# Scatters and early gathers six in a row with one wait, and the shared FFN's up-products of groups 2 to 15 as three products of high and low parts

## The reference, cut to what matters

```
gelu = lambda t: jax.nn.gelu(t, approximate=False)
shared = gelu(x @ W1s + b1s) @ W2s + b2s
rw = jax.nn.softmax(x @ Wr, axis=-1)
topw, topi = jax.lax.top_k(rw, K)                       # K = 2 of E = 8 experts
...
h = gelu(jnp.einsum('bsd,edf->bsef', x, W1p) + b1p)
priv = jnp.einsum('bsef,efd->bsed', h, W2p) + b2p
routed = jnp.einsum('bsed,bse->bsd', priv, mask)
return shared + routed
```

## Time and profile before

| | us |
|---|---|
| median of 3 runs (lowest, highest) | 1102.97 (1098.57, 1109.63) |
| the profiled execution, its own time | 1114.18 |
| its span | 1112.5 |
| shared FFN and routing, from the phase's first matmul to up-product 0 of the experts | 275.1 to 392.9 |
| expert tiles, to the last store's issue | 392.9 to 645.2 |
| graph phase and last FFN | 645.2 to 1112.5 |

### The profile page before, as it was taken

How to read it: one execution, slowest core, us unless ns; L and a number is a source line. 1 busy time by engine, 2 the same in 40 slices (tenths; PEclk the granted TensorE clock), 3 DMA queues, 4 the chain that set the end, 5 groups by cost and what they waited for, 6 DMA issues and landing times. The chain is left out here.

```text
span 1112.5 us, 25145 instructions
## 1 busy us (share of the span) xinstructions
PE 974.8 (88%) x7933; PEld 818.3 (74%) x7981; DVE 738.6 (66%) x2240; ACT 677.5 (61%) x1670; POOL 479.2 (43%) x477
## 2 busy tenths in 40 slices
PE   1699999897999999999899957998888998459998
PEld 1578888886677799999899934665556665349997
DVE  4689899885550155554455545788778896569998
ACT  4446666754433456666566625887677787367773
POOL 2556555551155654444444225666656312011111
PEclk9989999997999999999999978999999999679999
DMA  7902222112623146766576510111101000001111
GB/s 201 376 7 115 115 113 113 72 40 79 178 87 105 46 131 201 204 206 194 170 209 202 150 33 24 32 32 29 32 22 35 9 1 1 1 1 38 29 38 48
DMA packets 93001, 103.45 MB, mean 93 GB/s; under 512 B 16480, under 2 KB 69856, under 8 KB 90720
## 3 DMA queue, kind: packets, MB, share of 16 engines
q1 hardware_dynamic: 73232, 59.71, 16.5%
q10 hardware_dynamic: 11472, 25.63, 8.1%
q0 software_dynamic: 8192, 16.79, 5.0%
HBM read 52.54 MB, written 43.27 MB: 86 GB/s over the span
## 5 line engine op out<-in xcount | busy, mean ns | idle before, releaser
L1303 POOL DMA_INDIRECT slot_rows_in<-xn_all,slots x128 | 128.5, 1004 | 136.7 <-DMA slot_rows_in<-xn_all,slots 87.8
L1189 ACT ACTIVATE s_hT<-s_hp,expert 128x256 f32<-128x256 f32 x284 | 114.0, 474 | 72.0 <-PE s_hp L1180 51.2
L1202 PE MATMUL s_yp<-w_experts,s_hT 128*128 x1136 | 139.5, 276 | 1.7 <-issue 1.6
L1202 PEld LDWEIGHTS s_yp<-w_experts,s_hT 128*128 128x128 f32 x1136 | 133.8, 193 | 2.3 <-issue 2.3
L1210 DVE TENSOR_TENSOR xnT_all<-s_yp,expert 128x256 f32<-128x256 f32 x71 | 30.1, 423 | 117.3 <-PE s_yp L1202 87.2
L489 DVE SCALAR_TENSOR_TENSOR l_mi<-l_sbc,mT 128x512 bf16<-128x512 f32 x128 | 84.2, 668 | 5.7 <-PE l_sbc L480 5.0
L1178 PE MATMUL s_hp<-e_xh,e_wh 128*128 128x256 f32 x284 | 86.3, 304 | 0.0
L1101 ACT ACTIVATE s_hT<-s_hp,b_shared 128x512 f32<-128x512 f32 x64 | 44.0, 687 | 65.1 <-PE s_hp L1084 61.8
L1180 PE MATMUL s_hp<-e_xh,e_wl 128*128 128x256 f32 x284 | 80.7, 284 | 0.0
L1179 PE MATMUL s_hp<-e_xl,e_wh 128*128 128x256 f32 x284 | 80.6, 284 | 0.0
L1668 PE MATMUL g_hh<-w_fc,g_r1T 128*128 128x257 f32 x256 | 65.3, 402 | 14.5 <-ACT g_h L1683 9.0
(11 more groups left out here) (336 smaller groups left out, 2689.4 us busy)
## 6 DMA issues: line engine op xcount, KB each, us to landing
expert<-expert_rows ACTq DMA_DIRECT2D x65, 322.0 KB
slot_rows_in<-zeros SPq DMA_DIRECT2D x9, 1024.0 KB, 12.4
xnT_all<-slot_rows_in SPq DMA_DIRECT2D x71, 128.0 KB
slot_rows_out<-xnT_all SPq DMA_DIRECT2D x71, 128.0 KB
slot_rows_out<-zeros SPq DMA_DIRECT2D x8, 1024.0 KB, 4.4
xn_all<-l_xr SPq DMA_DIRECT2D x16, 256.0 KB
xnT_all<-l_rT SPq DMA_DIRECT2D x16, 256.0 KB
out_dram<-f_ot SPq DMA_DIRECT2D x16, 256.0 KB, 2.3
```

What stands on the lines that cost most here:

```text
L1189: nc.scalar.activation(hT[q % 2][:, c, :], hp[:, c, 0:TILE], ACT.Gelu, bias=wt[q][:, F + c:F + c + 1]).then_inc(s["h_ok"], 1)
L1202: ins = pe.matmul(yp[q % 2][:, h * D:(h + 1) * D], hT[q % 2][:, c, h * P:(h + 1) * P], w2, start=(c == 0 and h == 0), stop=(c == FC - 1), ...
L1303: pool.indirect_dma_start(k.rows_in, bass.IndirectOffsetOnAxis(ap=k.slots[:, c, b:b + 1], axis=0), k.xn[:, b, :], None).then_inc(scattered ...
```

## The change: scatters, gathers and up-products

One semaphore takes the place of the two of the scatters, and one that of the early gathers. POOL waits before every sixth transfer until all earlier ones have landed and issues six without a wait; the fences move to those places. In the shared FFN the up-products of groups 0 and 1 stay in float32. For groups 2 to 15 ACT rounds the group's tokens to fp32r (`act_shared_high`), VectorE takes the difference (`dve_shared_low`), and TensorE makes three fp32r products of 512 columns for each quarter. The shared weights are split once, into `wh[0]` and `wl[0]`. Those buffers belong to the expert tiles too, so ACT splits the first expert's weights only once the last shared up-product is through.

```diff
@@ pe_shared_up
+            if g >= SPLIT:
+                wait(pe, s["sxl_ok"], g - SPLIT + 1)
             for c in range(FC):
                 wait(pe, s["sh_ok"], (g - 1) * FC + c + 1)
-                pe.matmul(hp[:, c, :], k.w1_shared[:, c * P:(c + 1) * P],
-                          k.xnT[:, bass.ds(g * GB, GB), :], start=True, stop=True).then_inc(s["sh_ps"], 1)
+                at = slice(c * P, (c + 1) * P)
+                if g < SPLIT:
+                    ins = pe.matmul(hp[:, c, :], k.w1_shared[:, at], k.xnT[:, g * GB:(g + 1) * GB, :],
+                                    start=True, stop=True)
+                else:
+                    pe.matmul(hp[:, c, :], wh[0][:, at], xh[g % 2][:], start=True, stop=False)
+                    pe.matmul(hp[:, c, :], wh[0][:, at], xl[g % 2][:], start=False, stop=False)
+                    ins = pe.matmul(hp[:, c, :], wl[0][:, at], xh[g % 2][:], start=False, stop=True)
+                ins.then_inc(s["sh_ps"], 1)
...
+        def act_shared_high(act, g):
+            wait(act, s["sh_ps"], (g - 1) * FC if g - 2 >= SPLIT else 0)
+            nc.scalar.copy(xh[g % 2][:], group_of(k.xnT, g)).then_inc(s["sxh_ok"], 1)
+
+        def dve_shared_low(dve, g):
+            wait(dve, s["sxh_ok"], g - SPLIT + 1)
+            dve.tensor_tensor(xl[g % 2][:], group_of(k.xnT, g), xh[g % 2][:].bitcast(F32), ALU.subtract)\
+                .then_inc(s["sxl_ok"], 1)
@@ gpsimd, scatters (the early gathers in the same way)
+                arrived = 0
                 for n in range(TOPK * BATCHES):
                     b, c = n // TOPK, n % TOPK
-                    wait(pool, scattered[c], 16 * b)
                     if n % IN_A_ROW == 0:
-                        wait(pool, scattered[1 - c], 16 * b)
-                    if c == 0 and b % CHUNK == 1 and b > 1:
-                        pool.memset(pool_fence[:, b // CHUNK - 1:b // CHUNK], 0.0).then_inc(s["arrived"], 1)
+                        wait(pool, scattered, 16 * n)
+                        if n >= (arrived + 1) * TOPK * CHUNK:
+                            pool.memset(pool_fence[:, arrived:arrived + 1], 0.0).then_inc(s["arrived"], 1)
+                            arrived += 1
@@ scalar
+                nc.scalar.copy(wh[0][:], k.w1_shared[:]).then_inc(s["swh_ok"], 1)
+                for g in range(SPLIT, SPLIT + 2):
+                    act_shared_high(act, g)
+                for g in range(GROUPS - 1):
+                    act_shared_gelu(act, g, g % 2)
+                    if SPLIT <= g < GROUPS - 2:
+                        act_shared_high(act, g + 2)
+                act.wait_ge(s["sh_ps"], GROUPS * FC)
                 for q in range(2):
                     act_w_high(act, 0, q)
@@ vector, in the routing
+                dve.wait_ge(s["swh_ok"], 1)
+                dve.tensor_tensor(wl[0][:], k.w1_shared[:], wh[0][:].bitcast(F32), ALU.subtract)
+                dve_shared_low(dve, SPLIT)
                 dve_shared_add(dve, 0, 0)
...
+                dve_shared_low(dve, SPLIT + 1)
...
                 dve_shared_add(dve, 3, 1)
+                dve_shared_low(dve, 6)
...
-                for i in range(2, GROUPS // 2 - 1):
-                    for p in range(2):
-                        dve_shared_add(dve, i * 2 + p, p)
+                for g in range(4, GROUPS - 2):
+                    dve_shared_add(dve, g, g % 2)
+                    if g + 3 < GROUPS:
+                        dve_shared_low(dve, g + 3)
```

More of the change, by code:

```diff
@@ L1021, in experts_phase @@
         yt = [k.xnT[:, H * (U + q):H * (U + q) + H, :] for q in range(U)]
-        xh, xl = [[sb(f"e_x{c}{p}", [P, TILE], F32R) for p in range(2)] for c in "hl"]
+        xh, xl = [[sb(f"e_x{c}{p}", [P, GB * P], F32R) for p in range(2)] for c in "hl"]
         wh, wl = [[sb(f"e_w{c}{p}", [P, F], F32R) for p in range(2)] for c in "hl"]
@@ L1033, in experts_phase @@
             "iota", "d", "slots", "keys", "marks", "table", "tot_ps", "pre_ps", "key_ps", "tab_ps", "arrived",
-            "sh_ps", "sh_ok", "sy_ps", "sy_read", "fold",
+            "swh_ok", "sxh_ok", "sxl_ok", "sh_ps", "sh_ok", "sy_ps", "sy_read", "fold",
             "tp_ps", "xh_ok", "xT_ok", "wh_ok", "wl_ok", "h_ps", "h_ok", "y_ps", "y_ok")}
         rows_kept = sem("m_rows_kept")
-        scattered = [sem(f"m_scattered{p}") for p in range(2)]
-        early = [sem(f"m_early{c}") for c in range(TOPK)]
+        scattered, early = sem("m_scattered"), sem("m_early")
         x_in = [sem(f"m_x_in{q}") for q in range(U)]
@@ L1177, in pe_up @@
                 at, out_c = slice(c * P, (c + 1) * P), hp[:, c, 0:TILE]
[L1178 to L1180 removed]
+                pe.matmul(out_c, wh[q % 2][:, at], xh[q % 2][:, 0:TILE], start=True, stop=False)
+                pe.matmul(out_c, wh[q % 2][:, at], xl[q % 2][:, 0:TILE], start=False, stop=False)
+                pe.matmul(out_c, wl[q % 2][:, at], xh[q % 2][:, 0:TILE], start=False, stop=True).then_inc(s["h_ps"], 1)
         def act_gelu(act, i, q):
@@ L1317, in _ @@
                         pool.tensor_tensor(gather_fence[:, at:at + 1], k.ones[:, 0:1], k.ones[:, 0:1], ALU.mult)
-                    wait(pool, early[c], 16 * b)
                     if n % IN_A_ROW == 0:
-                        wait(pool, early[1 - c], 16 * b)
+                        wait(pool, early, 16 * n)
                     pool.indirect_dma_start(
                         slot_rows(k, c, b), None, k.rows_out,
-                        bass.IndirectOffsetOnAxis(ap=k.slots[:, c, b:b + 1], axis=0)).then_inc(early[c], 16)
-                for c in range(TOPK):
-                    pool.wait_ge(early[c], 16 * CHUNK * EC)
+                        bass.IndirectOffsetOnAxis(ap=k.slots[:, c, b:b + 1], axis=0)).then_inc(early, 16)
+                pool.wait_ge(early, 16 * TOPK * CHUNK * EC)
             @block.scalar
             def _(act):
-                for g in range(2):
-                    act_shared_gelu(act, g, g)
-                for i in range(1, GROUPS // 2 - 1):
-                    for p in range(2):
-                        act_shared_gelu(act, i * 2 + p, p)
-                act_shared_gelu(act, GROUPS - 2, 0)
+                nc.scalar.copy(wh[0][:], k.w1_shared[:]).then_inc(s["swh_ok"], 1)
[6 more added lines that the diff above has]
+                act.wait_ge(s["sh_ps"], GROUPS * FC)
                 for q in range(2):
@@ L1497, in _ @@
                 fold(dve.tensor_copy(k.w_f2_hand[:], fold_2[:, 1:2].to_broadcast([P, P])))
-                for i in range(2, GROUPS // 2 - 1):
-                    for p in range(2):
-                        dve_shared_add(dve, i * 2 + p, p)
-                dve.wait_ge(s["sh_ps"], -(-2 * H * U // GB) * FC)
+                for g in range(4, GROUPS - 2):
+                    dve_shared_add(dve, g, g % 2)
+                    if g + 3 < GROUPS:
+                        dve_shared_low(dve, g + 3)
+                dve.wait_ge(s["sh_ps"], (GROUPS - 1) * FC)
                 dve_w_low(dve, 0, 0)
```

16 lines of the change are left out of this document (11 added, 5 removed).

## The result

| | before | changed |
|---|---|---|
| median (lowest to highest), 4 runs each | 1103.85 us (1098.57 to 1109.63) | 1156.17 us (1149.52 to 1163.44) |
| ratio of the runs, 95% interval | | 1.0457 (1.0397 to 1.0517) |
| span of the profiled execution | 1112.5 us | 1147.4 us |
| first shared product to first expert product | 117.7 us | 115.7 us |
| first expert product to the last high x high product of tile 70 | 247.6 us | 300.3 us |

I forecast 1095.7 us, and 1087 to 1108. The medians are 52.3 us apart, and the two lower lines of the table say where the loss lies: the shared FFN is 2.0 us shorter, the expert tiles are 52.7 us longer. The spans differ by 34.9 us only.

What follows compares the result with a forecast made beforehand. TensorE was taken to bound shared FFN and expert tiles. Of 3.4 us saved in groups 2 to 6, 1.1 remain; groups 7 to 15 bring 6.2, together 7.3: 1102.97 - 7.3 = 1095.7 us, range 1087 to 1108.

Steps and rivals of the forecast that it cites:

- tiles 3.44 us apart throughout: Expert tiles: sign that the new profile would show every tile 3.44 us after the one before.
- the scatters' step: POOL's scatters among the tiles: six take 11.5 us instead of 13.0, all in at 533 us (528 to 552).
- more than forecast: Rival, expert tiles: earlier scatters end late landings behind TensorE's missing 4.4 us, giving 1091 us; chance 0.12.
- Late loads: Rival, expert tiles: six scatters in flight delay SP's tile loads; at 12.5 us a load, 1115 us; chance 0.08.
- The scatters as the bound: Rival, expert tiles: six scatters still take 13.0 us, tile 48 comes no sooner, no change, 1103 us; chance 0.15.
- the period of 6.35 us: Shared FFN: up-products plus down-products of a group take 6.3 us, each of groups 2 to 15 saving 0.69 us.
- the waits for VectorE before up(6) and up(7): Shared FFN, end of routing: TensorE waits 1.7 and 1.0 us for low parts of groups 6 and 7, not later.
- the handover: Shared FFN to expert tiles: ACT splitting the first experts' weights after the last up-product costs nothing.
- The shared stage: Shared FFN: the split up-products save 7.3 us in sum at the last up-product.
- Six scatters among tiles: Expert tiles: six scatters without inner waits take 11.5 us, between bounds of 11.1 and 13.0.

Runs made afterwards that it cites:

- e1: Kernel before with only the scatters and early gathers six in a row, up-products left in float32, chip B: 1.0645 of the kernel before.
- e3: Changed kernel with two semaphores again, both waited for at every sixth transfer, no wait inside a six, chip B: 1.0354 of the kernel before.
- e13: Changed kernel unaltered, as control on chip E: 1.0490 of the kernel before.
- e14: Changed kernel with one tiny POOL operation behind each scatter and early gather, six in a row, chip E: 1.0306 of the kernel before.
- e16: Changed kernel with three tiny POOL operations behind each scatter and early gather, six without a wait, chip B: 0.9979 of the kernel before.
- e15: Changed kernel with each scatter taking only the first 16 partitions' rows, six in a row, chip E: 1.1429 of the kernel before.
- e9: Changed kernel unaltered, as control on chip D: 0.9959 of the kernel before.
- e2: Changed kernel with the old two semaphores and waits, so the split up-products alone, chip B: 1.0015 of the kernel before.
- e4: Changed kernel with three transfers in a row and a full wait at every third, chip B: 0.9990 of the kernel before.
- e17: Changed kernel with three tiny POOL operations behind each transfer, except the first 24 scatters, chip D: 1.0068 of the kernel before.
- e5: Changed kernel with one tiny POOL operation behind each scatter and early gather, six in a row, chip C: 0.9933 of the kernel before.
- e7: Changed kernel with each scatter taking only the first 16 partitions' rows, six in a row, chip C: 0.9929 of the kernel before.

## Why the prediction was wrong

**The step that failed** is the one that I never priced: "tiles 3.44 us apart throughout". In the scatters' step I reckoned what closer issue does for POOL (11.1 to 13.0 us for six) and what the transfers do to the tiles' loads, and set its effect on the other engines' instructions at nothing. On the chip of the result it costs 52.7 us in the tiles. e1 and e3 show that the missing waits do it; e13, e14 and e16 that it hangs on how closely POOL issues; e15 that it isn't the bytes. On chips C and D the step holds (tiles 3.43 us apart in e9).

**It stood in the profile of before.** I read the 4.4 us that TensorE lacks in the earlier trace rows as late landings, and made a gain of them ("more than forecast"). They were mostly one stall at 542 to 548 us, behind five scatters 1.26 us apart: a small sample of what the change makes of many runs. One look at what TensorE waited for ("issue"), and at POOL at the same time, would have made a rival of it on the slower side. The quiet piece that I did look at (372.63 to 381.94) has the same pace of scatters without a stall, and so I took the pace for harmless.

**Late loads**, my rival on the slower side, had the right sign and place and the wrong mechanism: no transpose waited for a load between 388 and 562 us. The lower share of the DMA engines in the tiles (0.50, and 0.65 in the earlier trace rows) is a consequence: fewer tiles were worked on.

**The scatters as the bound** (0.15) is real where POOL keeps a slow pace: tile 48 waits 4.7 us in e2, 4.9 in e4, 8.9 in e16, 7.4 in e17. The last fence stands 166 to 169 us behind the first expert product in these four; in the kernel before it was 552.4 - 392.9 = 159.5 us. The wait costs e2's tiles 7.0 us, and is why the up-products alone give nothing.

**Right were:** the period of 6.35 us (6.3), the waits for VectorE before up(6) and up(7), 1.42 and 1.07 us (1.7 and 1.0), nothing later, and no cost at the handover. The shared stage gave 5.4 to 6.5 us wherever the down-products did not stutter (117.7 less 111.2 to 112.3), 7.3 forecast: a period saves 0.66 us, not 0.69. In the run of the result 4 us of it went, 3.5 in two stutters of the down-products that begin at 357 and 366 us and 0.7 in a gap at 378 us. Six scatters among tiles that don't stutter took 10.7 us (e9, the mean from scatter 72 to 120), not 11.5.

**What stays open:** what a closely issued transfer of POOL's and TensorE's instructions have in common, and which part of the transfer it is (POOL's instruction, its packets or its 16 increments); whether TensorE's instructions ("issue") or the increments between engines ("remote") are held up first; why the first six runs of six pass without a gap; and what sets chips B and E and that of the result apart from C and D. The distance inside a run and the mean pace aren't separated: six took 9.3 to 10.6 us in the tiles of the runs with full-size scatters that lost 3% and more, 12.2 and more in e2, e4 and e16. A profile of before on a calm chip wasn't taken.

## What to carry to other kernels

A wait between the indirect transfers of POOL may be worth more than it costs: it spaces them. Before taking such waits away, look at TensorE's "issue" gaps and the others' "remote" waits wherever POOL already issues four or five in a row. One stutter there is a warning, and one quiet run no proof of the opposite. And a comparison needs its control on the same chip: e5 to e7 looked like cures until e9 ran.

## What the runs showed of the hardware that I had not expected

- On some chips POOL's indirect transfers, 1.26 us apart, cut TensorE to 930 products in 160 us (1331 before); 1.15 us apart and with an eighth of the rows, to 17 in 50 us (439 on chip D). 1.66 us and more apart they caused no stall (e16, chip B).
- The same program takes 1087.7 us on chip D and 1174.8 us on chip E, 8% more, while the kernel before differs by 1.7% (1093.7 and 1111.9 us).
- The granted clock falls with the gaps, to 0.89 over 393 to 553 us and to 0.50 (1.2 GHz) in e15, and adds to the loss: up-products stand 0.43 us apart at 487.56 us of e15, clock 0.50, and 0.23 us at 494.63, clock 1.00.
